# Query weights split on GpSimd's own transfers, and four double tiles of 17 as three fp32r passes, in a Perceiver layer

## The chip, the cores and the metric

The kernel runs on one core of a Trainium2 chip. The core has a TensorE (PE) for matrix products, a VectorE (DVE), a ScalarE (ACT) and a GpSimd (POOL), and a SyncE (SP) that here only issues transfers; 16 DMA engines move data between HBM and the on-chip memories SBUF and PSUM. The engines run their own instruction streams and meet at semaphores. The metric is the device time of one execution in microseconds (us), lower is better.

## The reference, cut to what matters

Three layers follow each other, all in fp32: cross-attention, a decayed linear attention, and a small mixture of LoRA experts. The change touches the first and the hand-over to the second.

```python
# x: 1 x 256 x 1024, context: 1 x 4096 x 1024, 32 heads of 128, 4 key/value heads
latents = _layernorm(x)
hidden  = concatenate([context, latents])            # 4352 rows
q = latents @ Wq                                     # 32 heads
k = hidden @ Wk;  v = hidden @ Wv                    # 4 heads, each shared by 8 query heads
scores = einsum("bqhgd,bkhd->bhgqk", q, k) / sqrt(128)
out = einsum("bhgqk,bkhd->bqhgd", softmax(scores), v)
x = x + out.reshape(256, 4096) @ Wo
x = x + linear_attention(_layernorm(x));  x = x + lora_mixture(_layernorm(x))
```

## The kernel before, in words

**Arithmetic.** A product that wants fp32 accuracy is made in one of two ways. Plain: one fp32 matmul, which the profile records as two TensorE instructions. Split: each operand a is held as hi (a rounded to fp32r) and lo (a - hi), and `three_pass` (L111) adds hi*hi, hi*lo and lo*hi in three fp32r matmuls. A split costs a copy on ScalarE or GpSimd (hi) and a subtraction on VectorE or GpSimd (lo).

**Stage 1** (`project_keys_values`, about 0 to 387 us). The context comes in eight chunks of 512 columns. For each, TensorE makes the keys of the four key/value heads (`keys`, L423) and the values of four 128-row tiles (`values`, L433). ScalarE copies keys to `k_hi` (L326), which has two buffers: the copy of head g waits until the store of head g - 2 has landed (`k_stored`). VectorE makes `k_lo` (L379) and TensorE may start on a head's PSUM bank again only when that is done. Keys and values go to scratch in HBM.
Beside this, the query weights (16 pairs of heads, 1 MB a pair) are split once: SP loads a pair into `wq_raw` (L264), GpSimd makes hi (`tensor_copy`, L364) and lo (`tensor_tensor`, L366), and SP stores both (L260, L262). All of these transfers stand in SP's one queue, written out by hand in `split_query` and `store` (L256 to L281): `split_query` waits for GpSimd, and the key stores of the chunk stand behind it. hi and lo of a pair live in `hT_hi`, `hT_lo`; the LayerNorm of the latents writes there too, so ScalarE waits for all 32 stores before it (L354), and SP does before it loads the first weights of the next stage (L310). The program loads `x` once, in stage 1, and keeps it for the residual.

**Stage 2** (`cross_attention`, about 387 to 1374 us). The work goes in 16 pairs n of heads, 512 queries a pair (2 heads x 256). The 4352 keys are 17 double tiles j of 2 x 128. While pair n multiplies its probabilities with the values, pair n + 1 makes its scores, interleaved by hand in `pe_slot` (L938): two double tiles of scores first (`LEAD`), then for each j the values of j (`pe_values`, L907: two plain fp32 matmuls of 128x128 by 128x512, v against the exponentials) and the scores of j + 2 (`pe_scores`, L873: two `three_pass`), then the query projection of pair n + 3 (`pe_query`). In this text V_j is the start of the values of double tile j. The other engines follow with the same j:
- VectorE: `dve_shift` of double tile j + 1 (L803, scores less their maximum), then `dve_peak` of the next pair's j (L782).
- ScalarE: `act_exp` of j + 1 (L662) into a ring `probs` of three (`KEEP`), then `act_row` of the next pair's j (L644), which copies scores out of PSUM and lets TensorE make the scores of j + 2. `act_exp` waits until the values and GpSimd's addition of double tile j + 1 - 3 are done.
- GpSimd: `pool_add` (L715, L718) adds each double tile of exponentials to `sums`, 16 additions a pair, and three smaller steps: `pool_sum_low` after j = 3 (L730), `pool_output` after j = 11 (L737), `pool_sum` at the end (L725).

Pairs 0 to 14 overlap with the scores of the next one; the last pair has only its own values. Four slots form a loop body (`slots`, L562). `load_values` (L589) brings the values of a key/value head in four pieces, one transfer a piece.

**Stage 3** (`project_out`, about 1374 to 1472 us) multiplies with Wo in 16 steps and adds the residual; while it runs, SP fetches the first weights of the linear attention in four halves (`load_first_pair`).

Of the kernel before, what the change touches and what calls it, by code (L numbers as in the profile page):

```python
# [31 lines left out]
P = 128  # L32
# [171 lines left out]
def project_keys_values(nc, x, ctxT, wk, wv, wq, x_sb, hT_hi, hT_lo, ident, ones, k_drams, v_dram, wq_drams, shared):  # L204
# [5 lines left out]
    with ExitStack() as ctx:  # L210
        a = Alloc(nc, ctx, "kv_")
        w_raw = a.sb("w_raw", [P, KT, KVH * D])
# [43 lines left out]
        def split_query(sp, m, load=True):  # L256

            if m is not None:
                sp.wait_ge(wq_hi_ready, m)
                sp.dma_start(wq_drams[0][bass.ds(m - 1, 1)].rearrange("h p k d -> p (h k) d"), f32(hT_hi[:, :, :])).then_inc(wq_stored, 16)  # L260
                sp.wait_ge(wq_lo_ready, m)
                sp.dma_start(wq_drams[1][bass.ds(m - 1, 1)].rearrange("h p k d -> p (h k) d"), f32(hT_lo[:, :, :])).then_inc(wq_stored, 16)  # L262
            if load:
                sp.dma_start(wq_raw, wq[bass.ds(0 if m is None else m, 1)].rearrange("h p k d -> p (h k) d")).then_inc(wq_in, 16)  # L264

        def store(sp, c, tiles, pairs=None):

            n = tiles * P
            for g in range(KVH):
                if pairs is not None and g == KVH - 1:  # L270
                    split_query(sp, pairs)
# [5 lines left out]
            if pairs is not None:  # L277
                split_query(sp, pairs + 1)
# [5 lines left out]
        def _(sp):  # L284
# [12 lines left out]
            sp.wait_ge(w_lo_ready, 2 * KT)  # L297
            sp.sem_inc(wq_stored, 32)
            split_query(sp, None)
# [7 lines left out]
            split_query(sp, PAIRS, False)  # L307
            store(sp, NCHUNK - 3, VT)
            store(sp, NCHUNK - 2, VT)
            sp.wait_ge(wq_stored, 32 * (PAIRS + 1))  # L310
# [24 lines left out]
        def _(act):  # L335
# [18 lines left out]
            act.wait_ge(wq_stored, 32 * (PAIRS + 1))  # L354
# [126 lines left out]
KEEP = 3  # L481
# [12 lines left out]
def cross_attention(nc, wq_drams, k_drams, v_dram, hT_hi, hT_lo, ident, ones, oT_dram, shared, proj, last_pair):  # L494
# [9 lines left out]
    with ExitStack() as ctx:  # L504
        a = Alloc(nc, ctx, "xa_")
        kT_hi, kT_lo = shared.r
        v = a.sb("v", [P, KV])
        more_rows = a.sb("rows", [P, J - ENDS[0], 2, W])
        rows = [carve(shared.f, 2 * W * j, 2, W) for j in range(ENDS[0])] + [more_rows[:, j] for j in range(J - ENDS[0])]
        probs = [carve(shared.stage, 2 * W * i, 2, W) for i in range(2)] + [a.sb("probs", [P, 2, W])[:, :, :]]  # L510
# [9 lines left out]
        ident_r = a.sb("ident_r", [P, P], F32R)  # L520
        ones_r = a.sb("ones_r", [P, P], F32R)
        rounded = a.sem("rounded")
        max_q = a.sb("max_q", [P, W // P], F32R)
        o_raw = a.sb("o_raw", [P, W])
        inverse = a.sb("inverse", [P, W])
# [9 lines left out]
        v_in = [a.sem(f"v_in{i}") for i in range(len(ENDS))]  # L535
        q_done = a.sem("q_done")
# [52 lines left out]
        def load_values(sp, g, i):  # L589
            at = piece_columns(i)  # L590
            sp.dma_start(v[:, at], v_dram[bass.ds(g, 1)].rearrange("g p t d -> (g p) (t d)")[:, at]).then_inc(v_in[i], 16)
# [1238 lines left out]
```

## Time and profile before

| | |
|---|---|
| time before, median of 3 runs | 2005.69 us (2005.5 to 2009.59) |
| the profiled execution | 2007.68 us, of which 2005.9 us span |
| granted TensorE clock, mean over the span | 0.995 |
| PE busy | 98% of the span |
| DVE, ACT, POOL busy | 61%, 47%, 40% of the span |
| stages 1, 2 and 3 | about 387, 987 and 98 us; the rest is the linear attention and the mixture |

The span is the time between the first and the last instruction that the profile records. A busy engine means that an instruction was open on it; TensorE's instructions overlap (a record of 0.39 us may be followed by the next one after 0.23 us), so the pace of TensorE is read from start to start, not from durations. "Idle before <- X" names what an engine waited for. PEld is the loading of weights into TensorE, which overlaps its matmuls. SPq rows are transfers that SP issues, with the time that the issue took.

### The profile page before, as it was taken

How to read it: one execution, taken by the hardware profiler on the slowest of the kernel's cores; microseconds unless marked ns; L12 is line 12 of the kernel's file. 1: busy time of each engine (PE TensorE's matmuls, PEld its weight loads, DVE VectorE, ACT ScalarE, POOL GpSimd, SP SyncE). 2: the span in 40 equal slices, each digit the busy share in tenths (PEclk: the TensorE clock that was granted, in tenths of full speed). 3: DMA queues.
4: the chain of work that ended last, by engine and by line, in shares of the span. 5: the costliest groups of instructions: out<-in, count | busy, mean ns of one | idle time of the engine just before them, and what ended most of it. 6: DMA issues, size and time to landing. Idle time of an engine off the chain costs nothing. (4 is left out here: it accounts for less than half of the span.)

```text
span 2005.9 us, 26987 instructions
## 1 busy us (share of the span) xinstructions
PE 1965.8 (98%) x9725; PEld 1519.4 (76%) x9725; DVE 1222.2 (61%) x1294; ACT 951.1 (47%) x1015; POOL 810.0 (40%) x362
## 2 busy tenths in 40 slices
PE   9999999999999999999999999998999999999998
PEld 7887888876666666666666666545899999999886
DVE  4312221157877777877777877787756666666555
ACT  3112110055665655665665665664635544455442
POOL 2444320016766767766767766783000000000200
PEclk9999999999999999999999999999999999999999
DMA  8888873430123210321112210015735554444462
GB/s 306 305 311 324 325 292 147 147 123 1 48 95 106 71 49 6 110 98 63 49 48 95 79 61 1 6 58 188 272 137 189 188 185 178 176 176 178 145 235 88
DMA packets 72225, 283.86 MB, mean 142 GB/s; under 512 B 6400, under 2 KB 24320, under 8 KB 56512
## 3 DMA queue, kind: packets, MB, share of 16 engines
q1 hardware_dynamic: 72128, 282.65, 38.7%
q8 instruction: 51, 0.84, 0.2%
q14 instruction: 46, 0.38, 0.1%
HBM read 212.89 MB, written 69.73 MB: 141 GB/s over the span
## 5 line engine op out<-in xcount | busy, mean ns | idle before, releaser
L718 POOL TENSOR_TENSOR xa_sums<-xa_sums,stage 128x1024 f32<-128x1024 f32 x150 | 362.8, 2419 | 39.1 <-ACT stage L662 33.1
L916 PE MATMUL xa_o_ps<-stage,xa_v 128*128 128x512 f32 x768 | 360.4, 592 | 4.0 <-ACT stage L662 4.0
L782 DVE TENSOR_TENSOR xa_peak<-xa_s_ps,xa_peak 128x1024 f32<-128x1024 f32 x224 | 273.1, 1219 | 71.6 <-PE xa_s_ps L115 70.8
L113 PE MATMUL xa_s_ps<-xa_qT_hi,split 128*128 128x512 f32 x544 | 304.2, 559 | 5.7 <-issue 3.0
L644 ACT ACTIVATE xa_rows<-xa_s_ps 128x1024 f32<-128x1024 f32 x208 | 213.4, 1026 | 101.9 <-DVE xa_peak L782 70.1
L803 DVE TENSOR_TENSOR xa_rows<-xa_rows,xa_r_ps 128x1024 f32<-128x1024 f32 x208 | 248.2, 1195 | 0.0
L916 PEld LDWEIGHTS xa_o_ps<-stage,xa_v 128*128 128x128 f32 x768 | 143.6, 189 | 115.7 <-issue 98.6
L718 POOL TENSOR_TENSOR xa_sums<-xa_sums,xa_probs 128x1024 f32<-128x1024 f32 x75 | 179.0, 2386 | 124.7 <-ACT xa_probs L662 122.1
L115 PE MATMUL xa_s_ps<-xa_qT_hi,split 128*128 128x512 f32 x544 | 214.9, 395 | 0.0
L114 PE MATMUL xa_s_ps<-xa_qT_lo,split 128*128 128x512 f32 x544 | 213.0, 392 | 0.0
L662 ACT ACTIVATE stage<-xa_rows 128x1024 f32<-128x1024 f32 x144 | 152.4, 1060 | 65.4 <-DVE xa_rows L803 57.7
L1431 DVE TENSOR_TENSOR pair_lo<-pair_raw,pair_hi 128x4096 fp32r<-128x4096 f32 x30 | 132.8, 4426 | 81.3 <-ACT pair_hi L1368 81.3
L1358 POOL TENSOR_TENSOR square_sum<-square_sum,la_squares 128x512 f32<-128x512 f32 x16 | 20.8, 1299 | 385.7 <-ACT la_squares L1398 385.7
L113 PEld LDWEIGHTS xa_s_ps<-xa_qT_hi,split 128*128 128x128 f32 x544 | 102.4, 188 | 77.8 <-issue 40.9
L379 DVE TENSOR_TENSOR kv_k_lo<-kv_k_ps,kv_k_hi 128x512 fp32r<-128x512 f32 (+1 forms) x36 | 23.5, 659 | 221.8 <-ACT kv_k_hi L326 221.8
L326 ACT ACTIVATE kv_k_hi<-kv_k_ps 128x512 fp32r<-128x512 f32 (+1 forms) x36 | 20.4, 572 | 288.3 <-DMA kT_lo_scratch<-kv_k_lo 227.8
L916 PE MATMUL xa_o_ps<-xa_probs,xa_v 128*128 128x512 f32 x320 | 150.6, 593 | 2.2 <-ACT xa_probs L662 2.2
L114 PEld LDWEIGHTS xa_s_ps<-xa_qT_lo,split 128*128 128x128 f32 x544 | 102.7, 189 | 65.3 <-issue 52.1
L113 PE MATMUL la_qk_ps<-hT_hi,pair_hi 128*128 128x256 f32 x512 | 145.6, 284 | 0.3 <-PEq L1031 0.3
L115 PE MATMUL la_qk_ps<-hT_hi,pair_lo 128*128 128x256 f32 x512 | 144.8, 283 | 0.0
L114 PE MATMUL la_qk_ps<-hT_lo,pair_hi 128*128 128x256 f32 x512 | 144.7, 283 | 0.0
L115 PEld LDWEIGHTS xa_s_ps<-xa_qT_hi,split 128*128 128x128 f32 x544 | 102.0, 187 | 23.1
(305 smaller groups left out, 4599.8 us busy)
## 6 DMA issues: line engine op xcount, KB each, us to landing
pair_raw<-in_w_qk SPq DMA_DIRECT2D x15, 2048.0 KB, 7.7
pair_raw<-in_w_gv SPq DMA_DIRECT2D x15, 2048.0 KB, 7.8
kv_w_raw<-in_wq SPq DMA_DIRECT2D x16, 1024.0 KB, 7.9
wq_hi_scratch<-x_hT_hi SPq DMA_DIRECT2D x16, 1024.0 KB, 4.1
wq_lo_scratch<-x_hT_lo SPq DMA_DIRECT2D x16, 1024.0 KB, 5.0
full<-in_wo SPq DMA_DIRECT2D x16, 1024.0 KB, 5.3
pair_raw<-in_w_out SPq DMA_DIRECT2D x16, 1024.0 KB, 5.0
xa_w_hi<-wq_hi_scratch SPq DMA_DIRECT2D x15, 1024.0 KB, 4.8
```

The lines of the kernel that those rows point to most:

```text
L113: pe.matmul(out, w_hi, m_hi, start=first, stop=False)
L114: pe.matmul(out, w_hi, m_lo, start=False, stop=False)
L115: return pe.matmul(out, w_lo, m_hi, start=False, stop=last)
L379: dve.tensor_tensor(k_lo[:, g % 2, 0:n], k_ps[:, g, 0:n], f32(k_hi[:, g % 2, 0:n]), ALU.subtract).then_inc(k_copied, 1)
L644: act.activation(rows[j], s_ps[:, 2 * b:2 * b + 2, :], ACT.Copy).then_inc(row_ready, 1)
L662: act.activation(probs[j % KEEP], rows[j], ACT.Exp, scale=SCALE).then_inc(exp_done, 1)
L718: pool.tensor_tensor(sums[:, :, :], sums[:, :, :], probs[j % KEEP], ALU.add).then_inc(added, 1)
L782: dve.tensor_tensor(peak[:, :, :], s_ps[:, 2 * b:2 * b + 2, :], peak[:, :, :], ALU.max).then_inc(peak_done, 1)
L803: dve.tensor_tensor(rows[j], rows[j], r_ps[:, :].unsqueeze(1).to_broadcast([P, 2, W]), ALU.subtract).then_inc(shifted, 1)
L916: last = pe.matmul(o_ps[:, :], v[:, at], probs[j % KEEP][:, t, :], start=j == 0 and t == 0, stop=j == J - 1 and t == 1)
L1358: pool.tensor_tensor(square_sum[:, :, :], square_sum[:, :, :], squares[:, :, :], ALU.add).then_inc(sq_added, 1)
L1431: dve.tensor_tensor(w_lo[part][:, :, :], raw[part][:, :, :], f32(w_hi[part][:, :, :]), ALU.subtract).then_inc(w_lo_ready[part], 1)
```

## The change

**Stage 1.** SP no longer has the query weights in its queue. GpSimd issues the load and both stores of every pair itself, between its two computing instructions. `x` is loaded in stage 1 into a buffer of that stage and a second time in stage 3, ahead of the fourth of the prefetched halves; the residual waits for it.

**Stage 2.** Double tiles 2, 6, 10 and 14 (`SPLIT_STEPS`) of every pair but the last are multiplied in three fp32r passes instead of plain fp32. For this ScalarE takes the exponential a second time into `probs_hi` (fp32r), GpSimd subtracts it from the plain one (`pool_low`, into `probs_lo`) right after it has added that double tile, and TensorE waits for `low_by_pool`. The values of these four double tiles are split once for each key/value head (`act_values`, `dve_values`, in the slot u = 0). The ring of exponentials has four buffers, and shifts and exponentials run two double tiles ahead (`AHEAD`) instead of one. Pieces of values come in three transfers each. The last pair stays plain and reads plain copies of the four value tiles, loaded into the place of the query weights.

**Setup.** `ident` and `ones` are made as fp32r from the start, by two more casts on GpSimd at the very beginning in place of two at the start of stage 2. `inverse` shares the memory of `sum_row`.

```diff
@@ project_keys_values @@
-        def split_query(sp, m, load=True):
-            if m is not None:
-                sp.wait_ge(wq_hi_ready, m)
-                sp.dma_start(wq_drams[0][...], f32(hT_hi[:, :, :])).then_inc(wq_stored, 16)
-                sp.wait_ge(wq_lo_ready, m)
-                sp.dma_start(wq_drams[1][...], f32(hT_lo[:, :, :])).then_inc(wq_stored, 16)
-            if load:
-                sp.dma_start(wq_raw, wq[...]).then_inc(wq_in, 16)
...
                 load(sp, c + 2)
-                split_query(sp, 3 * c + 1)
-                store(sp, c, VT, 3 * c + 2)
+                store(sp, c, VT)
...
         def _(pool):
+            pool.wait_ge(w_lo_ready, 2 * KT)
             for m in range(PAIRS):
+                pool.dma_start(wq_raw, wq[m]).then_inc(wq_in, 16)
                 pool.wait_ge(wq_in, 16 * m + 16)
-                pool.wait_ge(wq_stored, 32 * m + 32)
+                if m:
+                    pool.wait_ge(wq_stored, 32 * m)
                 pool.tensor_copy(hT_hi[:, :, :], wq_raw).then_inc(wq_hi_ready, 1)
                 pool.wait_ge(wq_hi_ready, m + 1)
+                pool.dma_start(wq_drams[0][m], f32(hT_hi[:, :, :])).then_inc(wq_stored, 16)
                 pool.tensor_tensor(hT_lo[:, :, :], wq_raw, f32(hT_hi[:, :, :]), ALU.subtract).then_inc(wq_lo_ready, 1)
+                pool.wait_ge(wq_lo_ready, m + 1)
+                pool.dma_start(wq_drams[1][m], f32(hT_lo[:, :, :])).then_inc(wq_stored, 16)
@@ cross_attention @@
-KEEP = 3
+SPLIT_STEPS = (2, 6, 10, 14)
+KEEP = 4
+AHEAD = 2
...
             act.activation(probs[j % KEEP], rows[j], ACT.Exp, scale=SCALE).then_inc(exp_done, 1)
+            if j in SPLIT_STEPS and not last:
+                i = SPLIT_STEPS.index(j)
+                if i > 0:
+                    act.wait_ge(pv_done, J * n + SPLIT_STEPS[i - 1] + 1)
+                elif not first:
+                    act.wait_ge(pv_done, J * (n - 1) + SPLIT_STEPS[-1] + 1)
+                act.activation(probs_hi[:, :, :], rows[j], ACT.Exp, scale=SCALE).then_inc(probs_hi_ready, 1)
+
+        def act_values(act, g, j):
+            act.wait_ge(v_in[piece_of(j)], values_loaded(piece_of(j), g))
+            act.activation(v_hi[:, split_columns(j)], f32(v_lo[:, split_columns(j)]), ACT.Copy).then_inc(v_hi_ready, 1)
...
+        def pool_low(pool, n, j):
+            pool.wait_ge(exp_done, J * n + j + 1)
+            pool.wait_ge(probs_hi_ready, SPLIT * n + SPLIT_STEPS.index(j) + 1)
+            pool.tensor_tensor(probs_lo[:, :, :], probs[j % KEEP], f32(probs_hi[:, :, :]), ALU.subtract).then_inc(low_by_pool, 1)
...
+        def dve_values(dve, g, j):
+            at = split_columns(j)
+            dve.wait_ge(v_hi_ready, SPLIT * g + SPLIT_STEPS.index(j) + 1)
+            dve.tensor_tensor(v_lo[:, at], f32(v_lo[:, at]), f32(v_hi[:, at]), ALU.subtract).then_inc(v_lo_ready, 1)
...
+            if j in SPLIT_STEPS and not last_slot:
+                if values is not None:
+                    pe.wait_ge(v_lo_ready, SPLIT * values + SPLIT_STEPS.index(j) + 1)
+                pe.wait_ge(low_by_pool, SPLIT * n + SPLIT_STEPS.index(j) + 1)
+                for t in range(2):
+                    at = slice(split_columns(j).start + t * P, split_columns(j).start + (t + 1) * P)
+                    last = three_pass(pe, o_ps[:, :], v_hi[:, at], v_lo[:, at], probs_hi[:, t, :], probs_lo[:, t, :],
+                                      False, False)
+                last.then_inc(pv_done, 1)
+                return
@@ setup and project_out @@
+                pool.tensor_copy(ident_r[:, :], eye)
+                pool.tensor_copy(ones_r[:, :], one)
...
         def load_first_pair(sp, i):
+            if i == 3:
+                sp.dma_start(x_sb[:, :, :], x).then_inc(x_in, 16)
             weights.load_half(sp, i // 2, i % 2)
```

## Rows read from the trace of the kernel before

**Rows 1.** The page: busy time, share of the span and instructions of each engine.

```profile
PE 1965.8 (98%) x9725; PEld 1519.4 (76%) x9725; DVE 1222.2 (61%) x1294; ACT 951.1 (47%) x1015; POOL 810.0 (40%) x362
```

**Rows 2.** Windows: from:to us, length, then busy time of PE, PEld, DVE, ACT, POOL.

```profile
0.00:100.00 100.00, 97.36 (x429) 81.31 (x430) 36.52 (x56) 27.43 (x36) 33.37 (x15) 1.00 0.82 305
...
796.61:856.48 59.87, 59.87 (x229) 38.90 (x229) 45.37 (x43) 36.66 (x37) 42.23 (x19) 1.00 0.33 114
```

**Rows 3.** Timeline of PE in a slot: start, length (us), instruction.

```profile
804.28 1.88 PE L916 MATMUL xa_o_ps<-stage,xa_v 128*128 128x512 f32 x4
...
841.96 1.88 PE L916 MATMUL xa_o_ps<-stage,xa_v 128*128 128x512 f32 x4
...
843.90 0.39 PE L114 MATMUL xa_s_ps<-xa_qT_lo,split 128*128 128x512 f32 x1
...
845.06 1.88 PE L916 MATMUL xa_o_ps<-stage,xa_v 128*128 128x512 f32 x4
```

**Rows 4.** Timeline of POOL in the same slot.

```profile
800.32 2.40 POOL L715 TENSOR_TENSOR xa_sums<-stage 128x1024 f32<-128x1024 f32 x1 [6.47 <-ACT stage L662]
...
809.28 2.39 POOL L718 TENSOR_TENSOR xa_sums<-xa_sums,stage 128x1024 f32<-128x1024 f32 x1
811.63 1.30 POOL L730 TENSOR_TENSOR xa_sum_lo<-xa_sum_row,xa_sum_hi 128x512 fp32r<-128x512 f32 x1
812.88 2.38 POOL L718 TENSOR_TENSOR xa_sums<-xa_sums,stage 128x1024 f32<-128x1024 f32 x1
815.34 2.39 POOL L718 TENSOR_TENSOR xa_sums<-xa_sums,xa_probs 128x1024 f32<-128x1024 f32 x1
```

**Rows 5.** Timeline of ACT in the same slot: the exponential of double tile 5.

```profile
813.74 1.06 ACT L662 ACTIVATE xa_probs<-xa_rows 128x1024 f32<-128x1024 f32 x1 [0.78 <-DVE xa_rows L803]
```

**Rows 6.** Timeline of PE in stage 1: the three matmuls that waited longest.

```profile
151.16 0.50 PE L113 MATMUL kv_k_ps<-kv_c_hi,kv_wk_hi 128*128 128x512 f32 x1 [1.31 <-DVE kv_k_lo L379]
...
195.97 0.50 PE L113 MATMUL kv_k_ps<-split,kv_wk_hi 128*128 128x512 f32 x1 [0.96 <-DVE kv_k_lo L379]
...
241.02 0.50 PE L113 MATMUL kv_k_ps<-kv_c_hi,kv_wk_hi 128*128 128x512 f32 x1 [1.19 <-DVE kv_k_lo L379]
```

**Rows 7.** Timelines of ACT and of SP's queue ahead of the first of them.

```profile
149.78 0.60 ACT L326 ACTIVATE kv_k_hi<-kv_k_ps 128x512 fp32r<-128x512 f32 x1 [31.85 <-DMA kT_lo_scratch<-kv_k_lo]
...
137.66 0.33 SPq L262 DMA_DIRECT2D wq_lo_scratch<-x_hT_lo  x1
...
138.81 0.70 SPq L274 DMA_DIRECT2D kT_hi_scratch<-kv_k_hi  x1
```

**Rows 8.** Timeline of POOL in stage 1: the query weights (3 of 32 rows).

```profile
33.00 4.87 POOL L364 CAST x_hT_hi<-kv_w_raw 128x2048 fp32r<-128x2048 f32 x1 [31.36 <-DMA kv_w_raw<-in_wq]
...
131.06 1.90 POOL L364 CAST x_hT_hi<-kv_w_raw 128x2048 fp32r<-128x2048 f32 x1 [8.47 <-DMA kv_w_raw<-in_wq]
133.04 4.60 POOL L366 TENSOR_TENSOR x_hT_lo<-kv_w_raw,x_hT_hi 128x2048 fp32r<-128x2048 f32 x1
```

**Rows 9.** Timelines of SP's queue and of ACT at the end of stage 1.

```profile
318.66 0.50 SPq L312 DMA_DIRECT2D split<-wq_hi_scratch  x1
...
323.58 0.34 SPq L274 DMA_DIRECT2D kT_hi_scratch<-kv_k_hi  x1
...
345.22 2.07 ACT L194 ACTIVATE x_hT_hi<-kv_k_ps 128x512 fp32r<-128x512 f32 x4 [5.34 <-PE kv_k_ps L183]
```

**Rows 10.** Timeline of DVE and POOL in the last pair.

```profile
1357.87 3.09 DVE L821 TENSOR_TENSOR xa_peak<-xa_peak,stage 128x1024 f32<-128x1024 f32 x1 [1.58 <-ACT stage L662]
...
1359.83 2.26 POOL L737 TENSOR_TENSOR head_out<-xa_o_raw,xa_inverse 128x512 f32<-128x512 f32 x1
```

**Rows 11.** Timeline of POOL: one of the casts at the start of stage 2.

```profile
386.76 0.29 POOL L761 CAST xa_ident_r<-ident 128x128 fp32r<-128x128 f32 x1 [112.03 <-POOLq L210]
```

**Rows 12.** Timeline of ACT and PE in stage 3, after the fourth prefetched half.

```profile
1415.45 0.63 ACT L1012 ACTIVATE split<-split 128x512 fp32r<-128x512 f32 x1 [3.59 <-DMA split<-oT_scratch]
...
1419.48 0.50 PE L113 MATMUL wo_y_ps<-split 128*128 128x512 f32 x1 [0.26 <-DVE split L1021]
```

More of the change, by code:

```diff
@@ L491, in starts_piece, with plain_columns, split_columns, value_runs @@
     return j == 0 or j in ENDS
-def cross_attention(nc, wq_drams, k_drams, v_dram, hT_hi, hT_lo, ident, ones, oT_dram, shared, proj, last_pair):
+def plain_columns(j0, j1):
+    back = sum(s < j0 for s in SPLIT_STEPS)
+    return slice(2 * P * (j0 - back), 2 * P * (j1 - back))
+def split_columns(j):
+    i = SPLIT_STEPS.index(j)
+    return slice(2 * P * i, 2 * P * (i + 1))
+def value_runs(i):
+    runs, start = [], ENDS[i - 1] if i else 0
+    for j in range(start, ENDS[i]):
+        if j in SPLIT_STEPS:
+            if start < j:
+                runs.append((start, j))
+            runs.append((j, j + 1))
+            start = j + 1
+    if start < ENDS[i]:
+        runs.append((start, ENDS[i]))
+    return runs
+def cross_attention(nc, wq_drams, k_drams, v_dram, hT_hi, hT_lo, ident, ident_r, ones_r, oT_dram, shared, proj, last_pair):
     with ExitStack() as ctx:
@@ L600, in sync_slot @@
                 load_weight(sp, n + 3)
+            if last and u == 2:
+                sp.wait_ge(q_done, PAIRS)
+                load_last_values(sp)
             if not has_next:
@@ L690, in act_slot @@
                 act_output(act, n, not has_prev)
-                act_exp(act, n + 1, 0)
+                for j in range(AHEAD):
+                    act_exp(act, n + 1, j, last=last and u == 2)
         @block.scalar
@@ L699, in _ @@
                     act_query(act, 1, 1)
-            act_exp(act, 0, 0, True)
+            for j in range(AHEAD):
+                act_exp(act, 0, j, True)
             slots(act, act_slot)
@@ L841, in dve_slot @@
                 dve_max(dve, n + 1)
-                dve_shift(dve, n + 1, 0)
+                for j in range(AHEAD):
+                    dve_shift(dve, n + 1, j)
         @block.vector
@@ L852, in _ @@
             dve_max(dve, 0, True)
-            dve_shift(dve, 0, 0)
+            for j in range(AHEAD):
+                dve_shift(dve, 0, j)
             slots(dve, dve_slot)
@@ L905, in pe_spread, with pe_values @@
             last.then_inc(spread, 1)
-        def pe_values(pe, n, j, values, first):
+        def pe_values(pe, n, j, values, first, last_slot):
             if j == 0 and not first:
@@ L911, in pe_values @@
             if values is not None and starts_piece(j):
-                pe.wait_ge(v_in[piece_of(j)], 16 * (values + 1))
+                pe.wait_ge(v_in[piece_of(j)], values_loaded(piece_of(j), values))
+            if j in SPLIT_STEPS and not last_slot:
[8 more added lines that the diff above has]
+                return
             pe.wait_ge(exp_done, J * n + j + 1)
+            tile, start = (v_last, split_columns(j).start) if j in SPLIT_STEPS else (v, plain_columns(j, j + 1).start)
+            if j == SPLIT_STEPS[0]:
+                pe.wait_ge(v_last_in, 16 * SPLIT)
             for t in range(2):
-                at = slice((2 * j + t) * P, (2 * j + t + 1) * P)
-                last = pe.matmul(o_ps[:, :], v[:, at], probs[j % KEEP][:, t, :], start=j == 0 and t == 0,
+                at = slice(start + t * P, start + (t + 1) * P)
+                last = pe.matmul(o_ps[:, :], tile[:, at], probs[j % KEEP][:, t, :], start=j == 0 and t == 0,
                                  stop=j == J - 1 and t == 1)
@@ L934, in pe_sums_last @@
             for i, part in enumerate(pieces):
-                last = pe.matmul(t_ps[:, :], ones[:, :], part, start=i == 0, stop=i == len(pieces) - 1)
+                last = pe.matmul(t_ps[:, :], f32(ones_r[:, :]), part, start=i == 0, stop=i == len(pieces) - 1)
             last.then_inc(sum_spread, 1)
```

105 lines of the change are left out of this document (62 added, 43 removed).

## The prediction, made blind

> **What bounds the kernel now.** I read the page first. TensorE is busy 98% of the span and no other engine reaches two thirds [rows 1], so time is won where TensorE works less or waits less. Then the windows: in a slot of stage 2 (one pair of heads, 59.9 us) TensorE never idles, while VectorE, ScalarE and GpSimd are busy 45.4, 36.7 and 42.2 us [rows 2]. In the first 100 us it is 97.4% busy [rows 2]; the timeline of stage 1 has three waits on it, 1.31 + 0.96 + 1.19 = 3.5 us [rows 6].
>
> **Part 1, the products.** The timeline gives TensorE's pace. Values of one double tile start at 841.96, the next at 845.06: a step of 3.10 us [rows 3]. From the second scores pass (843.90) to 845.06 there are five fp32r passes, 0.232 us each; so the six passes of the scores take 1.39 us and the plain values 3.10 - 1.39 = 1.71 us. Three fp32r passes for both halves of a double tile are six more passes of the same shape, 1.39 us: a gain of 0.32 us. In stage 1, where nearly all of TensorE's work is such passes, 429 of them fill 97.36 us [rows 2], 0.227 us each; if the block of twelve ran so, the step would be 2.72 us and the gain 0.38. I take 0.34, near the measured pair. Four double tiles in 15 pairs: 60 x 0.34 = 20.4 us (19 to 23). TensorE is the bound there, so this lies on the path, if the others keep pace.
>
> **Part 2, GpSimd's pace in stage 2.** `pool_low` is a two-input pass over 128x1024, like the additions: 812.88 to 815.34, so 2.46 us from start to start [rows 4]. Four of them make its slot 42.2 + 9.8 = 52.0 us busy, of about 58.5. The average fits; the due times decide. GpSimd starts the slot at 800.32 with double tile 1 [rows 4]; with exponentials two ahead it need not pause after it. By the end of `pool_low` j it has done j additions, the lows so far, and the small steps: `pool_sum_low` adds 812.88 - 809.28 - 2.46 = 1.14 us [rows 4], `pool_output` I take as the same. TensorE wants it at V_j = 804.28 + 3.10 j, less 0.34 for each split before [rows 3]:
> j = 6: 800.32 + 8 x 2.46 + 1.14 = 821.1 against 822.5, early by 1.4.
> j = 10: 13 x 2.46, 833.4 against 834.6, early by 1.2.
> j = 14: 18 x 2.46 + 2.28, 846.9 against 846.7, late by 0.2.
> With a hand-over of 0.1 us TensorE waits 0.3 us at j = 14, 15 times: 4.5 us. After j = 14 GpSimd has two additions and `pool_sum`, 6.2 us, then some 6 us free before the next pair's first exponential [rows 4], so the lateness does not pile up. The bounds: 0 if the passes pack a little closer; for the other side each 0.1 us more in a pass costs 1.8 us a slot, and with 2.50 us a pass the wait is 1.0 us, 15 us in all. The waiting matmul has the scores of j = 16 behind it, and the peak and maximum of the next pair behind those; all slip by the same amount once.
>
> **Part 3, the other engines in a slot.** ScalarE gains four exponentials of 1.06 us [rows 5]: 36.7 + 4.2 = 40.9 of 58.5 us. Is it in time for GpSimd? At 813.74 it now makes the exponential of double tile 5 [rows 5]; running one further ahead, that place is tile 6's, and the second one ends at 815.9. GpSimd comes to addition 6 at 800.32 + 6 x 2.46 + 1.14 = 816.2, to its low at 818.7. So ScalarE is hidden, at cost 0; without that cover the price would be up to 4.2 us a slot. The ring of four with two ahead waits for double tile j - 2 at the same place of the stream as before, so it adds no wait either. VectorE's work is unchanged but for `dve_values`: four small subtractions in each of four slots, with both inputs in SBUF. Such an instruction and GpSimd get in each other's way: in the last pair one took 3.09 us while the 128x512 pass of GpSimd took 2.26 us [rows 10] instead of the 1.30 of the slot [rows 4]. Here VectorE's part is 128x256, about 0.4 us; three ahead of j = 14 make GpSimd 1.2 us later in those four slots, 4.8 us at most, 0 if they fall in a pause. I take 2. The Trainium skill (SBUF — State Buffer, "Who interferes with whom") says that such an instruction contends with a GpSimd instruction that reads SBUF, and that one fully waits for the other; by it the sum would have the 4.8. The trace agrees [rows 10]. The twelve transfers of values in place of four are issued on an SP queue that only waits there: 0. In the last pair nothing is split and GpSimd's 12 additions set the end: 0.
>
> **Part 4, stage 1.** The stall of rows 6 has this chain: the matmul waits for `k_lo`, that for ScalarE's copy at 149.78, that for the landing of a key store [rows 7]. SP issued the store at 138.81, directly behind the query stores, for which it had waited until 137.66 [rows 7]. With the query transfers off SP's queue, key stores go out when their keys are ready. I take the whole 3.5 us as gain (0 if the landing itself, under full DMA load, is what is late).
> GpSimd's chain has a due time instead. Per pair: load 8.0 us (of the 8.47 idle), cast 1.90, subtraction 4.60, hand-over 0.1 = 14.6 us [rows 8], plus three issues of t each. The first load can start at 33.00 - 8.0 = 25 [rows 8]. The last store lands some 5 us after 16 pairs: 25 + 16 x (14.6 + 3t) + 5 = 264 + 48t. SP needs that moment at 318.7 [rows 9], less the 3.5 gained: 315; some 4 us more are harmless, as TensorE needs the chunk's keys only near 345 [rows 9]. So t may be up to 1.15 us. The trace has no issue by GpSimd. Below, t is that of SP, 0.33 us [rows 7], which gives 280. Above, a cast of 1.90 us [rows 8] gives 355: SP would be held 36 us past 319, the last chunk's key stores behind it, and TensorE with them. I take 0.9, above SP's but nearer to it, so 307: cost 0. The Trainium skill (DMA: Bandwidth & Descriptors, "Latency and other measured facts") puts the first byte of a GpSimd-issued transfer at about 1 us against 0.6 us for SP's; an estimate from it is t = 0.33 + 0.4 = 0.73, also in time. No row of before shows it.
>
> **Part 5, the small ones.** Two casts of 0.29 us [rows 11] and two hand-overs move into the setup ahead of all transfers: +0.7 (0.5 to 1). Their old place was off the path. The second load of x (1 MB) comes in stage 3 where ScalarE already waited 3.59 us for a transfer and TensorE 0.26 us [rows 12]: +0.7 (0 to 3).
>
> **Sum.** -20.4 + 4.5 + 2 - 3.5 + 0.7 + 0.7 = -16.0 us. The profiled execution took 2007.7 us, 2.0 above the median of 2005.7; on the latter 1989.7, on the former 1991.7. I predict 1990. What a measurement of this kernel can tell from no change is 0.2%, 4 us.
>
> **The rivals.**
> A, GpSimd's transfers are too slow (ends slower). Place: the wait of SP for the last query store. Each 0.1 us of t past 1.15 costs 16 x 3 x 0.1 = 4.8 us. At t = 1.5 it is 17 us and the gain is gone; at 1.9 it is 36 us, 2026. For it: the rows bound t only between 0.33 and 1.90, and the queue of GpSimd is strictly in order. Against: 1.15 us is 3.5 times what an issue costs SP [rows 7]. A small lateness (1995 to 2002) 0.08, slower than before 0.08.
> B, GpSimd becomes the bound in stage 2. If a pass takes 2.55 us from start to start, the wait at j = 14 is 1.9 us a slot, 29 us in all: the time is 2014. It decides at 2.52 us a pass, where the wait is 1.4 us a slot and the whole sum is gone. For it: the last pair, where GpSimd runs without a pause, has longer passes beside VectorE. Against: in the slot the passes of rows 4 are packed and take 2.46. 0.09, of which 0.04 slower.
> C, everything fits: no wait at j = 14, no conflict, 0.38 a double tile: 2005.7 - 22.8 - 3.5 + 0.5 = 1980. 0.13.
> D, stage 1 gives nothing and the rest holds: 1993, inside my range.
>
> **How the numbers follow.** My forecast with its bounds (1983 to 1998) has 0.62, C 0.13, A 0.16, B 0.09. Slower by over 0.2%: 0.08 of A, 0.04 of B, 0.01 else: 0.13. Within 0.2%: 0.05. Faster 0.82. The range runs from 1981, near C, to 2002, the small lateness of A and half of B; below it C's last part and above it the slow cases remain, 2 in 10.
>
> **What would show it.** In the profile after: TensorE's steps with split double tiles 2.76 us long, the plain ones 3.10; slots of about 58.8 us; `pool_low` for j = 14 ending within 0.5 us of TensorE's wait on it, none at 2, 6 and 10; no wait of TensorE for `k_lo` near 150, 195 and 240; the last query store landed near 307 and SP not waiting for it. The prediction is wrong if GpSimd's issue costs over 1.15 us, if its passes slow down once they are packed, or if a ScalarE wait shows ahead of the additions.

## The result, and the profile after

The changed kernel takes 2013.87 us (median of 6 runs, 2011.46 to 2017.4), the kernel before, on the same chip, 2005.6 us (6 runs, 2004.23 to 2009.59). The ratio is 1.0032, 95% interval 1.0021 to 1.0042: slower, by 4 to 8 us, where 1990 us and a gain of 16 were forecast. The profiled execution of after took 2012.77 us, its span 2011.0, which is 5.1 more than the span before. The difference of the medians, 8.3 us, is larger; the rows explain the 5.1 us between the two profiled executions.

The page's first part, after (TensorE has 120 more matmuls and 15.5 us less to do; its share falls from 98% to 97%):

```profile
PE 1950.3 (97%) x9845; PEld 1537.3 (76%) x9845; DVE 1263.3 (63%) x1310; ACT 1006.5 (50%) x1091; POOL 986.6 (49%) x470
```

Windows of after, columns as in [rows 2]: the first 100 us, an ordinary slot, and the first slot of a group of heads.

```profile
0.00:100.00 100.00, 96.47 (x425) 80.56 (x426) 44.18 (x62) 32.15 (x39) 38.72 (x28) 1.00 0.80 303
852.60:911.97 59.37, 58.83 (x239) 40.22 (x238) 46.11 (x44) 39.93 (x41) 51.70 (x23) 1.00 0.20 68
912.00:974.90 62.90, 59.60 (x238) 39.92 (x238) 50.12 (x48) 41.36 (x45) 52.43 (x23) 1.00 0.13 48
```

The slot was 59.9 us [rows 2] and should have become 58.5. An ordinary one is 59.37, with 0.54 us in which TensorE idles; the first one of a group is 62.90, with 3.3 us of idling. GpSimd's 51.70 us and ScalarE's 39.93 are near what the prediction had, 52.0 and 40.9.

The 5.1 us add up over the stages. A slot is counted here from the matmuls that spread the maximum (L974, L903 before) to the next ones. Attention's first slot begins at 432.6 where it began at 437.3 (-4.7). Of these, 3.5 us are there at TensorE's last layernorm turn (340.97 after, 344.52 before); the rest fits the granted clock, which was 0.51 from 431 to 438 us before and 0.50 for only 3.4 us, from 427.9 to 431.3, in after. The first 15 slots take 900.7 us, and took 893.2 (+7.4). The last pair up to the first matmul of the output projection takes 46.2 and took 44.4 (+1.8), the rest 0.6 more.

Stage 1 first. Timeline of GpSimd's queue and passes in after, answering to [rows 8]:

```profile
44.08 0.58 POOL L354 DMA_DIRECT2D wq_lo_scratch<-x_hT_lo  x1 [0.30 <-POOL x_hT_lo L352]
44.65 0.53 POOL L345 DMA_DIRECT2D kv_w_raw<-in_wq  x1
56.50 1.90 POOL L349 CAST x_hT_hi<-kv_w_raw 128x2048 fp32r<-128x2048 f32 x1 [11.31 <-DMA kv_w_raw<-in_wq]
58.70 0.53 POOL L351 DMA_DIRECT2D wq_hi_scratch<-x_hT_hi  x1 [0.30 <-POOL x_hT_hi L349]
...
309.43 0.57 POOL L354 DMA_DIRECT2D wq_lo_scratch<-x_hT_lo  x1 [0.30 <-POOL x_hT_lo L352]
```

An issue takes GpSimd 0.53 to 0.58 us here, with 0.30 before each store, and the last one leaves at 309.43, before SP comes to the weights at 315.11. None of TensorE's three waits of [rows 6] is left.

Now the slot. Timeline of TensorE in after, steps 6 to 10 of an ordinary slot (step j is the time from V_j to V_j+1; the first matmul of each step's values; L1000 is a plain double tile, L113 the start of a split one):

```profile
878.72 0.40 PE L113 MATMUL xa_o_ps<-xa_probs_hi,xa_v_hi 128*128 128x512 f32 x1
...
881.46 1.88 PE L1000 MATMUL xa_o_ps<-xa_probs,xa_v 128*128 128x512 f32 x4
...
884.69 1.88 PE L1000 MATMUL xa_o_ps<-stage,xa_v 128*128 128x512 f32 x4
...
887.11 0.50 PE L113 MATMUL xa_s_ps<-xa_qT_hi,split 128*128 128x512 f32 x1 [0.54 <-ACT xa_rows L682]
...
888.60 1.88 PE L1000 MATMUL xa_o_ps<-stage,xa_v 128*128 128x512 f32 x4
...
891.71 0.39 PE L113 MATMUL xa_o_ps<-xa_probs_hi,xa_v_hi 128*128 128x512 f32 x1
```

From 878.72 to 881.46 the split step 6 takes 2.74 us, 0.36 less than the 3.10 of [rows 3]. Then step 7 takes 3.23, step 8 takes 3.91, step 9 takes 3.11. The shortened step is paid back, and more, in the next two. ScalarE's timeline shows what stands in the way at step 8:

```profile
884.14 1.06 ACT L700 ACTIVATE xa_probs<-xa_rows 128x1024 f32<-128x1024 f32 x1 [1.00 <-DVE xa_rows L864]
885.10 1.04 ACT L707 ACTIVATE xa_probs_hi<-xa_rows 128x1024 fp32r<-128x1024 f32 x1
886.05 1.00 ACT L682 ACTIVATE xa_rows<-xa_s_ps 128x1024 f32<-128x1024 f32 x1
```

The second exponential (L707) stands ahead of the row copy (L682), and it is this copy that frees the PSUM buffer for the scores at 887.11. In the first slot of a group it is worse. Timeline of VectorE in one, the subtraction for the values (it waits for ScalarE's rounding copy, then lasts 1.5 to 2.5 us), and under it the waits of TensorE in the same slot:

```profile
703.02 1.51 DVE L870 TENSOR_TENSOR xa_v_lo<-xa_v_lo,xa_v_hi 128x256 fp32r<-128x256 f32 x1 [1.33 <-ACT xa_v_hi L713]
...
716.52 2.48 DVE L870 TENSOR_TENSOR xa_v_lo<-xa_v_lo,xa_v_hi 128x256 fp32r<-128x256 f32 x1 [1.32 <-ACT xa_v_hi L713]
```

```profile
703.96 0.50 PE L113 MATMUL xa_s_ps<-xa_qT_hi,split 128*128 128x512 f32 x1 [0.85 <-ACT xa_rows L682]
708.72 0.50 PE L113 MATMUL xa_s_ps<-xa_qT_hi,split 128*128 128x512 f32 x1 [1.39 <-ACT xa_rows L682]
722.38 0.50 PE L113 MATMUL xa_s_ps<-xa_qT_hi,split 128*128 128x512 f32 x1 [0.94 <-ACT xa_rows L682]
```

From these rows I held that the order of work on ScalarE was the loss (my first theory), against rival A (GpSimd's transfers) and rival B (GpSimd's pace). It turned out to be the smaller part: run 2 below removes it alone.

### The profile page after: what moved, and what is told of

The parts are those of the page before. It is cut to its first block and busy times, and to the rows that moved or that the text cites. A ratio compares the mean times of both kernels' runs of the same rounds, so it can differ in the third digit from the quotient of the medians.

```text
span 2011.0 us, 27551 instructions
## 1 busy us (share of the span) xinstructions
PE 1950.3 (97%) x9845; PEld 1537.3 (76%) x9845; DVE 1263.3 (63%) x1310; ACT 1006.5 (50%) x1091; POOL 986.6 (49%) x470
## 5 line engine op out<-in xcount | busy, mean ns | idle before, releaser
L773 POOL TENSOR_TENSOR xa_sums<-xa_sums,xa_probs 128x1024 f32<-128x1024 f32 x120 | 292.7, 2439 | 21.3 <-ACT xa_probs L700 16.9
L113 PE MATMUL xa_s_ps<-xa_qT_hi,split 128*128 128x512 f32 x544 | 270.7, 498 | 23.4 <-ACT xa_rows L682 15.3
L1000 PE MATMUL xa_o_ps<-stage,xa_v 128*128 128x512 f32 x576 | 270.0, 592 | 3.9 <-ACT stage L700 3.9
L682 ACT ACTIVATE xa_rows<-xa_s_ps 128x1024 f32<-128x1024 f32 x208 | 212.6, 1022 | 98.4 <-DVE xa_peak L852 58.3
L773 POOL TENSOR_TENSOR xa_sums<-xa_sums,stage 128x1024 f32<-128x1024 f32 x105 | 252.5, 2405 | 16.8 <-ACT stage L700 10.7
L115 PE MATMUL xa_s_ps<-xa_qT_hi,split 128*128 128x512 f32 x544 | 213.5, 393 | 0.0
L113 PEld LDWEIGHTS xa_s_ps<-xa_qT_hi,split 128*128 128x128 f32 x544 | 102.2, 188 | 102.1 <-ACT xa_rows L682 46.7
L1000 PEld LDWEIGHTS xa_o_ps<-stage,xa_v 128*128 128x128 f32 x576 | 107.3, 189 | 87.1 <-issue 75.3
L700 ACT ACTIVATE stage<-xa_rows 128x1024 f32<-128x1024 f32 x112 | 118.5, 1059 | 67.9 <-DVE xa_rows L864 62.1
L113 PE MATMUL la_qk_ps<-hT_hi,pair_hi 128*128 128x256 f32 x512 | 145.6, 284 | 0.3 <-PEq L1114 0.3
L779 POOL TENSOR_TENSOR xa_probs_lo<-xa_probs,xa_probs_hi 128x1024 fp32r<-128x1024 f32 x60 | 145.5, 2425 | 0.0
L770 POOL TENSOR_TENSOR xa_sums<-stage 128x1024 f32<-128x1024 f32 x15 | 36.2, 2410 | 208.9 <-ACT stage L700 208.9
L700 ACT ACTIVATE xa_probs<-xa_rows 128x1024 f32<-128x1024 f32 x96 | 101.4, 1056 | 59.9 <-DVE xa_rows L864 55.1
```

The source lines that it names most:

```text
L113: pe.matmul(out, w_hi, m_hi, start=first, stop=False)
L115: return pe.matmul(out, w_lo, m_hi, start=False, stop=last)
L682: act.activation(rows[j], s_ps[:, 2 * b:2 * b + 2, :], ACT.Copy).then_inc(row_ready, 1)
L700: act.activation(probs[j % KEEP], rows[j], ACT.Exp, scale=SCALE).then_inc(exp_done, 1)
L770: pool.tensor_tensor(sums[:, :, :], probs[0], probs[1], ALU.add).then_inc(added, 1)
L773: pool.tensor_tensor(sums[:, :, :], sums[:, :, :], probs[j % KEEP], ALU.add).then_inc(added, 1)
```

## The experiments

Times are medians; "before" is the kernel before on the same chip as the run, and a ratio is to it. The changed kernel stands at 1.0032.

**1. Stage 1 alone.** The kernel before, with `split_query` taken off SP and GpSimd issuing the query transfers:

```
+            pool.wait_ge(w_lo_ready, 2 * KT)
             for m in range(PAIRS):
+                pool.dma_start(wq_raw, wq[m]).then_inc(wq_in, 16)
...
+                pool.dma_start(wq_drams[0][m], f32(hT_hi[:, :, :])).then_inc(wq_stored, 16)
```

> Kernel before, with only the query transfers of stage 1 moved to GpSimd. Theory (this part works, the loss is elsewhere): the three stalls of TensorE in stage 1 go, its last layernorm turn comes 3 to 4 us earlier as in the changed kernel (344.5 to 341.0), and nothing behind it changes: about 2002 us (2001.0 to 2003.0), 3.5 us under before. Rival A (GpSimd's transfers cost): no gain or a loss, 2005 us or more. If the 1 us later start of the changed kernel belongs to the set-up and not to this part, the first stage here gains up to 4.5 us.

Measured: 2002.85 us against 2007.61, ratio 0.9973 (0.9963 to 0.9983), so 3.4 to 7.4 us less. TensorE's last layernorm turn starts at 340.02, and was at 344.52; in the changed kernel it is at 340.97, because its set-up makes the first matmul later (8.99, was 8.10). Rival A is out, and the set-up costs 0.9 us as predicted (0.7).

**2 to 4. Three orders, one at a time, in the changed kernel.** ScalarE's second exponential behind the row copy:

```
                 if has_next:
                     act_row(act, n + 1, (u + 1 + j) % 2, j)
+                if j + AHEAD < J:
+                    act_exp_hi(act, n, j + AHEAD, not has_prev, not has_next)
```

> Changed kernel, with ScalarE's second exponential (for the high parts of a split double tile) put behind the row copy of the same step instead of ahead of it; nothing else. Theory (ScalarE's order of work is the loss): TensorE's waits for the row copies at step 8 (0.54 us each, with what they do to the step, 0.93 us a slot) go in about 14 slots, and part of those at j=0 of the last full slot: 10 to 14 us less than the changed kernel, 2000 to 2004 us. Rival B (GpSimd's pace bounds stage 2): within 2 us of the changed kernel, since GpSimd's passes stay as they are, 2012 to 2014.

The split of the values later, on ScalarE behind `act_row`, and on VectorE:

```
-                if u == 0 and j + 2 in SPLIT_STEPS:
-                    dve_values(dve, g, j + 2)
+                if u == 0 and j + 1 in SPLIT_STEPS:
+                    dve_values(dve, g, j + 1)
```

> Changed kernel, with the split of the values moved: ScalarE's rounding copy behind the row copy of its step, VectorE's subtraction a step later, so that it finds the copy done. Theory: VectorE's waits for ScalarE's copy (15.9 us over 13) go, and so do TensorE's waits for rows in the first slot of each group (about 3.5 us a slot in 3 to 4 slots): 7 to 12 us less than the changed kernel, 2002 to 2007 us; the ordinary slots stay at 59.4 us. If it is the conflict with GpSimd over memory that makes the subtraction 1.5 to 2.5 us long, and not the order, only 1 to 4 us come back. Rival B: within 1 us of the changed kernel.

GpSimd's low parts first:

```
-                    pool_add(pool, n, j, not has_prev)
                     if j in SPLIT_STEPS:
                         pool_low(pool, n, j)
+                    pool_add(pool, n, j, not has_prev)
```

> Changed kernel, with GpSimd's pass for the low parts ahead of its addition of the same double tile. Rival B (TensorE waits for GpSimd's low parts): they come 2.4 us earlier, and several us come back, 2005 to 2010. Theory: TensorE waits for them for 3.5 us in all, 1.5 of it in the slot without a query projection, so at most 1 to 3 us come back, and ScalarE may wait longer for the additions: 2011 to 2015.

Measured: 2009.74 (ratio 1.0004, 0.9995 to 1.0014), 2006.05 (0.999, 0.9981 to 1.0) and 2016.11 us (1.0038, 1.0024 to 1.0053), before 2007.61. The later values give some 8 us, as the theory had. Low parts first give nothing back as a whole (the intervals overlap); they help only in the slot without a query projection (57.7 to 55.8 us), while the first slots of a group grow from 62.9 to 65.0: rival B is out as the main cause. The row first gives 5 to 6 us where 10 to 14 were expected. (Its traced slots are only 1.3 us shorter in sum, but that execution, of 2014.0 us, is its slowest: in three stretches of 3.4 us the granted clock was 0.53 to 0.57, in slots 5, 8 and 12, counted from 0, and by the lengths of these slots that cost some 4 us.) The ordinary slots gain 0.2 us at most, and their timeline says why. TensorE with the row first, steps 7 to 11 of an ordinary slot:

```profile
883.32 1.88 PE L1004 MATMUL xa_o_ps<-xa_probs,xa_v 128*128 128x512 f32 x4
...
886.55 1.88 PE L1004 MATMUL xa_o_ps<-stage,xa_v 128*128 128x512 f32 x4
...
889.66 1.88 PE L1004 MATMUL xa_o_ps<-stage,xa_v 128*128 128x512 f32 x4
...
892.76 0.40 PE L113 MATMUL xa_o_ps<-xa_probs_hi,xa_v_hi 128*128 128x512 f32 x1
...
895.86 1.45 PE L1004 MATMUL xa_o_ps<-xa_probs,xa_v 128*128 128x512 f32 x3
```

Step 8 is 3.11 again (it was 3.91), but now the split step 10, from 892.76 to 895.86, takes 3.10 us and not 2.73: split or plain, the pace is the same. (A part of the gain also goes at step 13, which takes 3.2 to 3.5 us in ordinary slots: TensorE waits for the low parts of double tile 14, which GpSimd now gets later.) Something else sets the pace. VectorE's timeline of the kernel before, in the same steps:

```profile
883.42 0.96 DVE L811 RECIPROCAL xa_inverse<-xa_t_ps 128x128 f32<-128x128 f32 x1 [2.34 <-PE xa_t_ps L926]
884.29 1.16 DVE L803 TENSOR_TENSOR xa_rows<-xa_rows,xa_r_ps 128x1024 f32<-128x1024 f32 x1
885.37 1.21 DVE L782 TENSOR_TENSOR xa_peak<-xa_s_ps,xa_peak 128x1024 f32<-128x1024 f32 x1
886.50 0.95 DVE L811 RECIPROCAL xa_inverse<-xa_t_ps 128x128 f32<-128x128 f32 x1
...
889.57 0.95 DVE L811 RECIPROCAL xa_inverse<-xa_t_ps 128x128 f32<-128x128 f32 x1
...
892.64 0.95 DVE L811 RECIPROCAL xa_inverse<-xa_t_ps 128x128 f32<-128x128 f32 x1
```

VectorE waits 2.34 us for the spread sums, which TensorE makes only after the values of step 5. Then it has a reciprocal, a shift and a peak in each of four steps with hardly a gap, 3.07 us from one reciprocal to the next. TensorE's steps were 3.10 [rows 3], so VectorE kept up, by 0.03 us a step. A split step of 2.74 runs into it: the peak comes late, the row copy behind it, the scores behind that. This is the second theory: VectorE's pace in steps 6 to 10 is the bound that the change meets. It says what to try: the same work of VectorE, spread out.

**5. The reciprocals spread.** In the changed kernel:

```
-                if has_prev and 6 <= j < 10:
-                    dve_inverse(dve, n - 1, j - 6)
+                at = (7, 9, 11, 13) if has_next else (6, 7, 8, 9)
+                if has_prev and j in at:
+                    dve_inverse(dve, n - 1, at.index(j))
...
-                if has_prev and j == 11:
+                if has_prev and j == (15 if has_next else 11):
                     pool_output(pool, n - 1, 1 - u % 2, 8 * (n - u % 2) + 16)
```

> Changed kernel, with VectorE's four reciprocals on steps 7, 9, 11 and 13 in place of 6, 7, 8 and 9, and GpSimd's product that needs them at step 15 in place of 11, in all slots but the last. Theory, formed from the two runs before: with a reciprocal in each step VectorE needs 3.07 us a step (0.95, 1.16 and 1.21 us, overlapped), first waits 2.34 us for the spread sums, and so holds TensorE to its own pace from step 6 to 10; the shorter split steps 6 and 10 gain nothing there, and ScalarE's second exponential comes on top at step 8. Spread out, steps 7 and 8 come back to 3.10 us (from 3.23 and 3.91) in 14 slots: 10 to 14 us less than the changed kernel, 2000 to 2004 us. If ScalarE's order alone is the loss, as first thought, TensorE's 0.54 us waits stay and at most 2 us come back.

Measured: 1992.09 us against 2008.08, ratio 0.9919 (0.99 to 0.9937): 22 us less than the changed kernel, more than the theory had. Windows of this kernel, an ordinary slot:

```profile
842.70:901.10 58.40, 58.40 (x238) 40.35 (x237) 47.00 (x43) 39.74 (x42) 51.70 (x23) 1.00 0.25 90
```

The slot is 58.4 us, TensorE never idles, and VectorE and GpSimd have no less to do than in after (46.1 and 51.7 us). Timeline of TensorE, steps 6 to 10 (2.74, then 3.10 three times):

```profile
869.64 0.40 PE L113 MATMUL xa_o_ps<-xa_probs_hi,xa_v_hi 128*128 128x512 f32 x1
...
872.38 1.88 PE L1001 MATMUL xa_o_ps<-xa_probs,xa_v 128*128 128x512 f32 x4
...
881.68 0.40 PE L113 MATMUL xa_o_ps<-xa_probs_hi,xa_v_hi 128*128 128x512 f32 x1
...
884.42 1.88 PE L1001 MATMUL xa_o_ps<-xa_probs,xa_v 128*128 128x512 f32 x4
```

From step 6 to step 11 it is 14.78 us; with the row first it was 15.3, in after 15.7, before 15.5. ScalarE's order is that of after, and its 0.54 us wait is gone all the same: the second exponential did harm only where VectorE was late already. The first slots of a group are 59.0 us (62.9 in after), so most of their loss too was VectorE's subtraction coming on top of the reciprocals. VectorE in the ordinary slot of the rows above:

```profile
869.38 1.23 DVE L843 TENSOR_TENSOR xa_peak<-xa_s_ps,xa_peak 128x1024 f32<-128x1024 f32 x1 [0.75 <-PE xa_s_ps L115]
870.52 0.95 DVE L878 RECIPROCAL xa_sum_row<-xa_t_ps 128x128 f32<-128x128 f32 x1
...
875.68 1.23 DVE L843 TENSOR_TENSOR xa_peak<-xa_s_ps,xa_peak 128x1024 f32<-128x1024 f32 x1 [0.75 <-PE xa_s_ps L115]
876.82 0.95 DVE L878 RECIPROCAL xa_sum_row<-xa_t_ps 128x128 f32<-128x128 f32 x1
```

It waits for TensorE's scores again (0.75 us) every second step, and not for sums at all.

So the edit takes away two things at once, the late start and the run of four reciprocals. ScalarE's row copy of step 7 (L682), and the scores that use it, in after and here, show what the late start is worth:

```profile
882.12 1.02 ACT L682 ACTIVATE xa_rows<-xa_s_ps 128x1024 f32<-128x1024 f32 x1
...
883.20 0.50 PE L113 MATMUL xa_s_ps<-xa_qT_hi,split 128*128 128x512 f32 x1
```

```profile
870.64 1.03 ACT L682 ACTIVATE xa_rows<-xa_s_ps 128x1024 f32<-128x1024 f32 x1 [0.83 <-DVE xa_peak L843]
...
873.69 0.79 PE L113 MATMUL xa_s_ps<-xa_qT_hi,split 128*128 128x512 f32 x1
```

Counted from V_6 (878.72 and 869.64) the copy ends at 4.42 us in after and at 2.03 here. TensorE wants it at 2.74 + 1.71 = 4.45, the split step and the plain values that follow. In the kernel before (V_6 at 883.22, the copy from 886.62 to 887.64) it also ended at 4.42, against 3.10 + 1.71 = 4.81: 0.4 us to spare, of which the split of step 6 takes 0.36. The wait for the sums costs 2.4 us of lead. The pace alone, four steps of 3.07 against 2.74 + 3 x 3.10, would be behind by 0.24 us in all. By this estimate the late start weighs more than the pace, but no run has one without the other (reciprocals at steps 7, 8, 9 and 10 would), and GpSimd's product moved in the same edit.

**6 and 7. With the other orders on top.** Run 6 is 5 with the edit of 3, run 7 has those of 2 and 4 as well.

> The spread reciprocals and the later split of the values together. Theory: both gains add up, since the first slots of a group lose by VectorE's subtraction (1.4 to 2.5 us beside GpSimd) on top of its pace: 18 to 24 us less than the changed kernel, 1990 to 1996 us, the ordinary slots near 58.5 us and the first slot of a group within 1 us of them. If the subtraction still holds VectorE up, the first slots stay 2 us longer and it is 1996 to 2000.

> As the run before, and ScalarE's second exponential behind the row copy, and GpSimd's pass for the low parts ahead of its addition. Theory: with VectorE ahead of TensorE again the order on ScalarE matters little, except at step 0 of the last full slot: within 3 us of the run before, 1988 to 1997 us. If the low parts come too late (GpSimd starts them 1 us later, ahead of an addition), steps 1, 5, 9 and 13 grow past 3.2 us and it is 3 us or more above the run before.

Measured: 1991.01 us (ratio 0.9907, 0.9889 to 0.9926) and 1990.94 (0.991, 0.9893 to 0.9927), before 2008.08. Neither can be told from run 5. That the gains of 3 and 5 would add up was wrong: they take away the same wait. By the slots 6 gives 0.3 us in the first slots of groups; 7 takes the slot without a query projection from 56.3 to 54.7 and loses 1.2 in each first slot.

**8. No split at all.** The changed kernel with

```
-SPLIT_STEPS = (2, 6, 10, 14)
+SPLIT_STEPS = ()
```

> Changed kernel with no split double tile at all: all 17 go in fp32, as in the kernel before; the ring of four, ScalarE and VectorE two steps ahead, the transfers of stage 1, the set-up and the later load of x stay. Theory: the ring costs nothing, every ordinary slot is 59.93 us again, and what stays is stage 1's gain (5 us by the run with it alone) less the later start (1 us) and x (0.6 us): 2003 to 2006 us, so that the four splits together cost the changed kernel 8 to 11 us where they were to give 20. If the two steps ahead or the ring cost by themselves, 2008 us or more.

Measured: 2006.85 us against 2008.08, ratio 0.9996 (0.9983 to 1.0008), just above the 2003 to 2006 expected. The ordinary slots are 59.9 us. But the slot without a query projection is 55.7 where the kernel of run 1 has 54.6: TensorE waits 1.31 us for its first row copy, behind three exponentials and not two. So working two ahead costs about 1.1 us there. Four splits cost the changed kernel 7 us on balance; 8 to 11 were expected.

**9. The control: the edit of run 5 made in the kernel before.**

> Kernel before, with its four reciprocals spread over steps 7, 9, 11 and 13 and GpSimd's product at step 15, as in the run that took the changed kernel to 1992 us. Theory: with 17 fp32 double tiles TensorE needs 3.10 us a step, just over VectorE's 3.07 us with a reciprocal in it, so nothing is freed here: within 2 us of the kernel before, slots at 59.93 us. If spreading were worth something by itself (the 22 us gained were not the splits' own), 5 to 22 us less than before.

Measured: 2008.7 us against 2008.49, ratio 1.0003 (0.9994 to 1.0013), slots 59.93 us. What run 5 gained is not the worth of spreading by itself, but the splits' own gain, set free.

**10. Two splits, none in steps 6 to 10, reciprocals as they were.**

```
-SPLIT_STEPS = (2, 6, 10, 14)
+SPLIT_STEPS = (2, 14)
```

> Changed kernel with its reciprocals where they are, and two split double tiles (2 and 14) in place of four: none lies in the stretch of steps 6 to 10. Theory: both give their 0.36 us in each of 15 slots, VectorE's pace takes nothing back, so ordinary slots are 59.2 us, less than the 59.4 us of four splits, and the first slots of a group lose at most 1 us: 1995 to 1999 us, faster than with twice the splits. If splits lose by what they ask of GpSimd or of the memory, wherever they stand, half of the loss stays: 2004 to 2010 us.

Measured: 1997.85 us against 2008.49, ratio 0.9946 (0.9933 to 0.996), ordinary slots 59.2: half the splits, 17 us faster than all four. The first slots of a group still lose 0.9 us at step 13 (4.03), where the subtraction for double tile 14 meets GpSimd.

**11. The slot without a query projection.** Run 6, and in that one slot the first row copy ahead of the exponential, with the orders of 2 and 4:

```
+                late = last and u == 2
+                if late and j == 0:
+                    act_row(act, n + 1, (u + 1 + j) % 2, j)
                 if j + AHEAD < J:
...
+                early = last and u == 2 and j == 0
+                if early:
+                    dve_peak(dve, n + 1, (u + 1 + j) % 2, j)
                 if j + AHEAD < J:
                     dve_shift(dve, n, j + AHEAD)
```

> Spread reciprocals and later values, and in the last full slot, which has no query projection, the row copy and the peak of step 0 ahead of the exponential and shift of double tile 2, the second exponential behind the row copy and GpSimd's low parts ahead of its addition. Theory: that slot goes from 56.3 us to 54 (its step 0 from 5.46 to at most 4.5, steps 5, 9 and 13 lose their waits for low parts): 1 to 3 us less than the run without it, 1988 to 1990 us. If its wait is set by the way to the first row alone, the slot stays within 0.5 us.

Measured: 1988.03 us against 2008.49, ratio 0.9894 (0.9881 to 0.9907); the slot is 54.6 us (56.3 in run 6, 57.7 in after). It has the lowest median of all, 20 us under the kernel before (its interval still meets that of run 6), and it beats both kernels.

## Why the prediction was wrong

**Part 1** held: a split step is 2.74 us, 0.36 saved, within the bounds of 0.32 to 0.38; 60 of them are 21.6 us.

**Part 2** held in its pace, not in its wait of 4.5 us. GpSimd's passes for the low parts in after, from the page's costliest groups (count, busy us, mean ns):

```profile
L779 POOL TENSOR_TENSOR xa_probs_lo<-xa_probs,xa_probs_hi 128x1024 fp32r<-128x1024 f32 x60 | 145.5, 2425 | 0.0
```

They did not slow down once packed. TensorE waits long for them only in the slot without a query projection (0.44 and 1.49 us), so the 4.5 us of the sum were not needed; rival B did not happen. One reason stands in the rows of before: V_j = 804.28 + 3.10 j gives 841.5 for j = 12, and [rows 3] has 841.96. The formula left out the two matmuls that spread the sums after step 5, 0.46 us, and with them the low part of double tile 14 is early by 0.3 us instead of late by 0.2.

**Part 3 is the step that failed**, in the sentence "VectorE's work is unchanged but for `dve_values`". That is true of the amount, and the amount was no measure. I had summed VectorE over the slot (45.4 of 59.9 us [rows 2]) and never laid its work against the shorter steps. Ahead of step 7 it waited 2.34 us for the sums, and then in four steps it needed 3.07 of TensorE's 3.10 us; with a split step of 2.74 it is the bound there, through peak, row copy and scores. The whole row of [rows 2] and TensorE's timeline were read, VectorE's timeline in the slot was not. Moving those four reciprocals with the product that needs them, and nothing else, turns +6 into -16 us, each against the kernel before (ratios 1.0032 and 0.9919); in the kernel before the same edit gives nothing (run 9).

Two lesser errors stand in the same part. "ScalarE is hidden, at cost 0" was worked out against GpSimd, which reads the exponentials, and not against the row copy queued behind them; at step 8 it costs 0.8 us a slot, as run 2 shows, though in that run 0.37 of it is lost again at step 10 to VectorE's pace and 0.2 to 0.4 more at steps 13 and 14. And `dve_values`, put at 2 us and at most 4.8, was priced by its conflict with GpSimd's passes alone. It also waits for ScalarE's copy (15.9 us in all) and delays the peaks behind it: with the later split of values some 8 us came back.

The ledger of the 15 slots, from their lengths against 893.2 us less 21.6: ten slots lose 0.9 us each, one of them 1.4 (9.6 in all), three first slots of a group 4.45 (13.4), the first of all 1.45, the one without a query projection 4.6, in sum the 29.0 us seen. Run 5 has 877.6 us, 5.9 over that target; run 11 has 875.9.

**Part 4** held. GpSimd's issue takes 0.53 to 0.73 us, under the 0.9 taken and the limit of 1.15; the first slot begins 4.7 us earlier, and alone the part is worth 5.4 us (3.4 to 7.4), where 3.5 was taken. But GpSimd also idles 0.30 us before each store, and its loads took 8.8 us and not 8.0, so a pair takes 17.9 us where 17.3 was taken: the last store was to land near 307, it was issued at 309.43 and landed near 314, about 1 us before SP went on to the weights. The Trainium skill (DMA: Bandwidth & Descriptors, "Latency and other measured facts") gives when the first byte of a transfer comes, 1 us against 0.6; the estimate of 0.73 us for an issue took that difference for the engine's own time. The rows have 0.53 to 0.73 us, but they do not test the page's figure. Rival A did not happen.

**Part 5** held for the set-up (0.9 for 0.7) and for x: from the first matmul of the output projection to the first of the linear attention it takes 96.8 to 97.2 us with the second load (after, runs 5 and 10) and 96.1 in runs 1 and 9 without it, so 0.7 to 1.1 for 0.7; the traced execution of before had two other waits and 97.2. "In the last pair nothing is split", at cost 0, missed 1.8 us by the trace, and 1.5 of them are the granted clock. TensorE had waited 4.56 us when it came to the last sums:

```profile
1373.14 3.49 PE L1019 MATMUL xa_t_ps<-xa_sums,ones 128*128 128x512 f32 x4 [4.56 <-POOL xa_sums L814]
1376.42 2.08 PE L1019 MATMUL xa_t_ps<-xa_peak,ones 128*128 128x512 f32 x4
```

From 1373.14 to 1376.42, 3.28 us, the granted clock was 0.54, so mostly the lower of its two levels, 1.2 GHz; before, the same matmuls took 1.79 us (1370.31 to 1372.10) at 1.00. Run 1, which does not touch the last pair, has 45.9 us for this stretch too, with 3.4 us at a granted clock of 0.50 in it.

With VectorE spread out, the forecast of 1990 comes true at 1992.1, 1991.0 and 1990.9 us: the one large term that was missing is gone. That the numbers meet so closely is in part luck: run 5 does without the 4.5 and 2 us of the sum, but its slots still lose 5.9 us elsewhere, 3.1 of them in the slot without a query projection, for which the sum had no term.

## What to carry to other kernels

Before a step of the bounding engine is made shorter, lay every other engine's work against the new length of each step, and not its sum against the slot: an engine that is 76% busy on average may be 99% busy in the four steps that count, and a margin of 0.03 us shows as no wait at all. Look also for the place where such an engine waits for a result of the bounding engine with other work queued behind: here 2.34 us of waiting used up a lead of 2.4. A sign of it in the trace is an engine whose instructions follow each other with no idle time over several steps, after a long wait for the bounding engine. When work is added to an engine's queue, ask what stands behind it as well as who reads it; and if a change that should gain loses, try moving the work of the late engine before giving up the change.

## What was not expected of the hardware

A reciprocal of 128x128 from PSUM takes 0.95 us, a maximum over 128x1024 takes 1.21: for each of the elements in a row about six times as much, so that four small instructions filled the gap.

VectorE's instructions with two inputs in SBUF depend strongly on what GpSimd does beside them. The maximum of the two halves of the peak, 128x512, has a mean of 1.1 us before, 1.6 after, and 2.1 in run 2, where the pass for the low parts falls on it; the same shape with one input in PSUM takes 0.69 in all of them. The subtraction of 128x256 took 1.4 us on average and up to 2.5. The Trainium skill (SBUF — State Buffer, "Who interferes with whom") says that such pairs block each other for a whole instruction; the rows agree: in the slot of after shown above the maximum is open from 902.10 to 903.96, and the pass of GpSimd that had begun before it ends at 903.41, 0.55 us earlier; in run 2 it is 903.54 to 905.88 and 905.33, again 0.55. In run 5 it takes up to 2.54 us and TensorE does not wait for it in ordinary slots.

```profile
L846 DVE TENSOR_TENSOR xa_peak<-xa_peak 128x512 f32<-128x512 f32 x16 | 26.1, 1629 | 0.6
L870 DVE TENSOR_TENSOR xa_v_lo<-xa_v_lo,xa_v_hi 128x256 fp32r<-128x256 f32 x16 | 22.8, 1427 | 15.9 <-ACT xa_v_hi L713 15.9
```

The rows are VectorE's groups in after (count, busy us, mean ns, idle us before them).
